# Attention with minus the row maximum added in PSUM, and the state stage's weights prepared by GpSimd

## The reference

```
x = x + attention(_gn(x))
  win = windows of 7x7 pixels            # 16 images x 16 windows, 49 tokens each
  q, k, v = win @ w_qkv + b_qkv          # 4 heads of 8 channels
  attn = softmax(q @ k.T * 8**-0.5)      # 49 x 49 per window and head
  x1 = (attn @ v) @ w_proj + b_proj
x = x + state_stage(_gn(x))              # grouped 1x1, 3x3 depthwise conv,
                                         # in_proj, conv1d, x_proj, dt_proj,
                                         # scan over 784 steps, out_proj, ...
```

## Time and profile before

| | us |
|---|---|
| median of 3 runs | 478.54 |
| lowest, highest | 476.59, 478.87 |
| profiled execution, its own time | 475.85 |
| span of the profiled execution | 474.1 |

### The profile page before, as it was taken

One profiled execution on the slowest core, in us unless ns is written; L12 is line 12 of the kernel. 1 busy time (PEld: TensorE's weight loads), 2 busy tenths in 40 slices (PEclk: granted clock), 3 DMA queues, 4 the chain that ended last, 5 costly groups with the idle time before them and its releaser, 6 DMA issues. The chain is left out here.

```text
span 474.1 us, 10021 instructions
## 1 busy us (share of the span) xinstructions
PE 351.1 (74%) x3480; PEld 230.4 (49%) x3480; DVE 365.1 (77%) x679; ACT 299.8 (63%) x583; POOL 233.9 (49%) x217
## 2 busy tenths in 40 slices
PE   5149888896789785985877647666795829888885
PEld 4037676675665332142233213222483519877774
DVE  3799999999797388799787999997576685544443
ACT  4327788887785899578758946347985253333432
POOL 4526868775673324966972999567081130000000
PEclk9997999998899999599897885768999668999999
DMA  6110000000223231022000000000030000111111
...
DMA packets 24044, 10.29 MB, mean 22 GB/s; under 512 B 20576, under 2 KB 22368, under 8 KB 24016
## 3 DMA queue, kind: packets, MB, share of 16 engines
...
q0 software_dynamic: 128, 0.01, 0.2%
...
## 5 line engine op out<-in xcount | busy, mean ns | idle before, releaser
L480 POOL TENSOR_TENSOR Pr<-Pr,rc 128x392 f32<-128x392 f32 x64 | 54.4, 883 | 32.2 <-DVE rc L1826 32.2
L511 POOL TENSOR_TENSOR YA<-YA,hC 128x784 f32<-128x784 f32 x27 | 51.7, 1914 | 32.4 <-DVE hC L1910 31.5
L1349 PE MATMUL pair<-BCf,sel 96*128 96x392 bf16 x128 | 38.4, 394 | 35.0 <-DVE Hs L1894 30.8
L1894 DVE TENSOR_TENSOR_SCAN Hs<-dA,pair 128x784 f32<-128x784 f32 x32 | 57.1, 1785 | 1.0
L1193 PE MATMUL pair<-ident,Pr 128*128 128x128 f32 x256 | 41.1, 293 | 13.2 <-ACT PT L715 9.0
L1349 PEld LDWEIGHTS pair<-BCf,sel 96*128 96x128 bf16 x128 | 10.2, 105 | 74.0 <-issue 71.6
L1193 PEld LDWEIGHTS pair<-ident,Pr 128*128 128x128 f32 x256 | 29.2, 146 | 25.1 <-ACT PT L715 15.8
L1887 DVE TENSOR_TENSOR pair<-DU,pair 128x784 f32<-128x784 f32 x32 | 31.1, 973 | 10.6 <-PE pair L1349 10.3
L715 ACT ACTIVATE PT<-pair 128x392 f32<-128x392 f32 x64 | 31.4, 497 | 5.9 <-PE pair L1193 5.6
L724 ACT ACTIVATE Pr<-Ts 128x392 f32<-128x392 f32 x64 | 32.5, 536 | 3.4 <-DVE Ts L1810 3.4
L1804 DVE TENSOR_REDUCE mx<-pair 128x8 f32<-128x392 f32 x64 | 32.6, 550 | 1.6 <-PE pair L1150 1.4
...
## 6 DMA issues: line engine op xcount, KB each, us to landing
...
NB<-in_L_conv_x_proj_w SPq DMA_DIRECT2D x4, 3.0 KB
DW<-in_L_conv_dw SPq DMA_DIRECT2D x4, 1.1 KB
vec<-in_L_conv_b_qkv POOLq DMA_DIRECT2D x3, 0.5 KB, 5.8
...
```

Source lines behind the costliest of these rows:

```text
L480: eng.tensor_tensor(pg, pg, bcast(rc[:, g, :], 2, WT), ALU.mult).then_inc(pn_r, 1)
L511: eng.tensor_tensor(y, y, hC[:, n % NHC, :], ALU.add).then_inc(g_ya, 1)
L1349: ins = eng.matmul(SPREAD[s][:, columns(h)], sel[:, n, :], upper(BCf[:, c % 2, s, columns(h)]), start=True, stop=True)
L1894: eng.tensor_tensor_scan(Hs[:, n % 2, :], dA[:, n % NA, :], SPREAD[0], 0.0, ALU.mult, ALU.add).then_inc(v_s, 1)
```

## The change

The subtraction of the maximum leaves VectorE. The maxima of two groups (16 numbers a partition) are cut into an upper and a lower bf16 piece (`upper_piece`, `lower_piece`, into `MP`), TensorE turns them onto 32 rows of bank 7 (`turn_max`), VectorE copies these out as bf16 (`turned_max`, into `MT`), and a matmul of `MT` with a constant of 0 and -1 (`msel`) adds minus the maximum to the scores where they lie in PSUM (`shift`, with `start=False`). The exponential reads PSUM (`exponent`), and the banks are free for the next scores when the exponential is done (`exp_r` in place of `sub_r`). `Ts` is gone.

The weights of the state stage: GpSimd does the fifteen products into `W8X` and `NB` ahead of its first strip; VectorE keeps the block transpose, the mean and two small steps; GpSimd then makes the copies behind strip 0, `BD` behind strip 1 and `WBC` behind strip 2.

The diff, without changed declarations of semaphores and the waits `sub_r` to `exp_r` at the conv and delta matmuls:

```diff
--- before.py
+++ after.py
...
@@ -234,6 +236,11 @@
         s_out = [sem("s_out0"), sem("s_out1")]
 
         block = ctx.enter_context(nc.Block())
+
+        QP = 64 + WT
+
+        def shift_rows(part):
+            return banks[7][0:32, 256 + P * part:256 + P * part + QP]
 
         def strip(s):
             return bass.ds(s * ST, ST)
@@ -455,7 +462,23 @@
             eng.wait_ge(s_ev, 8)
             for m in (xw, Qw, Vst, Pr):
                 eng.memset(m[:], 0.0).then_inc(s_mk2, 1)
+            eng.memset(MT[:], 0.0).then_inc(s_mk2, 1)
+            eng.wait_ge(s_mk, 5)
+            eng.tensor_tensor(mrow[:, :], ident[0:32, 0:16], ident[0:32, 16:32], ALU.add).then_inc(s_mk2, 1)
+            eng.wait_ge(s_mk2, 6)
+            eng.tensor_scalar(msel[:, :, :, :].rearrange("p g m k -> p (g m) k"), bcast(mrow[:, :], 2, WT), -1.0, None, ALU.mult).then_inc(s_mk2, 1)
             eng.wait_ge(s_mk2, 1)
+            eng.wait_ge(s_sel, 1)
+            loaded(eng, 1)
+            for k, dst in ((0, W8X[:, :]), (1, NB[:, 1, :]), (2, NB[:, 2, :])):
+                ins = eng.tensor_tensor(dst.rearrange("p (h i) -> p h i", h=4), bcast(W8[:, k, :], 1, 4), bcast(mask8[:, :], 2, 8), ALU.mult)
+            ins.then_inc(s_hf, 1)
+            for k in range(3):
+                eng.tensor_scalar(NB[:, 4 + k, :], WIN[:, 0, :], C1[:, k:k + 1], None, ALU.mult)
+            eng.wait_ge(s_hf, 2)
+            for k in range(9):
+                ins = eng.tensor_scalar(NB[:, 7 + k, :], W8X[:, :], DW[:, k:k + 1], None, ALU.mult)
+            ins.then_inc(s_hf, 1)
 
             def pool_att(s, par):
                 nxt = not isinstance(s, int) or s + 1 < NS
@@ -479,8 +502,24 @@
                         pg = Pr[:, par, g, :, 0:WT]
                         eng.tensor_tensor(pg, pg, bcast(rc[:, g, :], 2, WT), ALU.mult).then_inc(pn_r, 1)
 
-            for s in (-1, 0, 1, 2):
-                pool_att(s, s % 2)
+            pool_att(-1, 1)
+            pool_att(0, 0)
+            eng.wait_ge(s_sel, 2)
+            eng.tensor_copy(W4[:, U_Z:U_DL, :], TB[:, 0:U_DL - U_Z, :]).then_inc(s_hf, 1)
+            for x in range(3):
+                rows = slice(C * x, C * x + C)
+                eng.wait_ge(s_hf, 4 + x)
+                eng.tensor_copy(W3[rows], TB[rows, U_DL - U_Z + x:16:3, :]).then_inc(s_hf, 1)
+            eng.wait_ge(s_hf, 7)
+            pool_att(1, 1)
+            eng.tensor_tensor(BD[:, U_Z:U_CV, :].rearrange("p u (g c) -> p u g c", g=G), bcast(W4[:, U_Z:U_CV, :], 2, G),
+                              bcast(bcast(bd[:, :], 1, U_CV - U_Z), 3, C), ALU.mult)
+            pool_att(2, 0)
+            for s in range(2):
+                for q in range(3):
+                    ins = eng.tensor_tensor(WBC[:, s, C * q:C * q + C].rearrange("p (g n) -> p g n", g=G),
+                                            bcast(TB[:, 17, R + DS * s:R + DS * s + DS], 1, G), bcast(bd[:, :], 2, DS), ALU.mult)
+            ins.then_inc(s_hf, 1)
             eng.memset(XP[:, :, :], 0.0).then_inc(s_bd, 1)
             with eng.Fori(0, 6) as it:
                 pool_att(it * 2 + 3, 1)
@@ -718,17 +757,17 @@
                 def exponent(g):
                     if not cur:
                         return
-                    eng.wait_ge(sub_r, 4 * s + g + 1)
+                    eng.wait_ge(sh_r, 4 * s + g + 1)
                     if not fixed or s >= 2:
                         eng.wait_ge(t_r, 4 * (s - 2) + g + 1)
-                    eng.activation(Pr[:, par, g, :, 0:WT], Ts[:, g, :, :], ACT.Exp).then_inc(exp_r, 1)
+                    eng.activation(Pr[:, par, g, :, 0:WT], banks[g][:, 0:392].rearrange("p (m k) -> p m k", k=WT), ACT.Exp).then_inc(exp_r, 1)
 
                 turned_out(0)
+                turned_out(1)
+                turned_out(2)
                 exponent(0)
-                turned_out(1)
+                turned_out(3)
                 exponent(1)
-                turned_out(2)
-                turned_out(3)
                 exponent(2)
                 exponent(3)
                 if nxt:
...
@@ -1150,8 +1189,25 @@
                                 ins = eng.matmul(banks[g][64 * half:64 * half + 64, 196 * pair:196 * pair + 196],
                                                  Qw[C * g:C * g + C, par, 2 * pair + half, :],
                                                  Km[C * g:C * g + C, par, 2 * pair + half].rearrange("p h k -> p (h k)"),
-                                                 start=True, stop=True)
+                                                 start=pair == 0, stop=False, skip_group_check=True)
                     ins.then_inc(s_r, 1)
+
+                def turn_max(part):
+                    if not cur:
+                        return
+                    eng.wait_ge(max_r, 10 * s + (5, 8)[part])
+                    if part == 0 and (not fixed or s >= 2):
+                        eng.wait_ge(ao_r, s - 1)
+                    eng.matmul(shift_rows(part), MP[:, part, :], upper(ident[:, 0:QP]), start=True, stop=True,
+                               skip_group_check=True).then_inc(mt_r, 1)
+
+                def shift(part):
+                    if not cur:
+                        return
+                    eng.wait_ge(max_r, 10 * s + 9 + part)
+                    for g in (2 * part, 2 * part + 1):
+                        eng.matmul(banks[g][:, 0:392], MT[:, part, :], msel[:, g % 2].rearrange("p m k -> p (m k)"),
+                                   start=False, stop=True, skip_group_check=True).then_inc(sh_r, 1)
 
                 scores(0)
                 scores(1)
@@ -1196,6 +1252,8 @@
                 def av():
 
                     eng.wait_ge(ring_r, base + G)
+                    if cur:
+                        eng.wait_ge(max_r, 10 * s + 10)
                     if not fixed or s >= 2:
                         eng.wait_ge(ao_r, s - 1)
                     for w in range(NW):
@@ -1209,11 +1267,16 @@
                 if prv:
                     transposes(0)
                     transposes(1)
+                turn_max(0)
                 if early:
                     early()
                 if prv:
                     transposes(2)
+                shift(0)
+                turn_max(1)
+                if prv:
                     transposes(3)
+                shift(1)
                 if prv2:
                     project()
                 if late:
...
@@ -1742,41 +1806,21 @@
                 return eng.tensor_tensor(BD[:, u0:u1, :].rearrange("p u (g c) -> p u g c", g=G), bcast(W4[:, u0:u1, :], 2, G),
                                          bcast(bcast(bd[:, :], 1, u1 - u0), 3, C), ALU.mult)
             eng.tensor_scalar(vec[:, V_BQS:V_BQS + 1], vec[:, V_BQ:V_BQ + 1], SCALE, None, ALU.mult)
-            eng.tensor_reduce(mask8[:, :], m16[:, :].rearrange("p (g h) -> p h g", g=G), AX.X, ALU.add)
+            eng.tensor_reduce(mask8[:, :], m16[:, :].rearrange("p (g h) -> p h g", g=G), AX.X, ALU.add).then_inc(s_sel, 1)
             spread_weights(U_Q, U_P + 1)
             gn_apply(0, lambda j: XN[:, T * j:T * j + T])
 
 
-            loaded(eng, 1)
-            link(eng.tensor_tensor(maskz[:, :], m8[:, 0:4], m8[:, 4:8], ALU.add))
-
-            for k, dst in ((0, W8X[:, :]), (1, NB[:, 1, :]), (2, NB[:, 2, :])):
-                ins = eng.tensor_tensor(dst.rearrange("p (h i) -> p h i", h=4), bcast(W8[:, k, :], 1, 4), bcast(mask8[:, :], 2, 8), ALU.mult)
-            link(ins)
-            for k in range(3):
-                eng.tensor_scalar(NB[:, 4 + k, :], WIN[:, 0, :], C1[:, k:k + 1], None, ALU.mult)
-            for k in range(9):
-                ins = eng.tensor_scalar(NB[:, 7 + k, :], W8X[:, :], DW[:, k:k + 1], None, ALU.mult)
-            link(ins)
+            eng.wait_ge(s_hf, 3)
             link(eng.transpose(TB[:, :, :].rearrange("p u c -> p (u c)"), NB[:, :, :].rearrange("p u c -> p (u c)")))
             assert chain[0] == TRB
 
             link(eng.tensor_reduce(omean[:, :], TB[:, 3, :], AX.X, ALU.add))
             link(eng.tensor_scalar(omean[:, :], omean[:, :], 1.0 / C, None, ALU.mult))
             link(eng.tensor_scalar(TB[:, 3, :], TB[:, 3, :], omean[:, 0:1], None, ALU.subtract))
-            eng.tensor_copy(W4[:, U_Z:U_DL, :], TB[:, 0:U_DL - U_Z, :])
-            link(eng.tensor_copy(W4[:, U_CV:NU, :], TB[:, U_DL - U_Z:16, :]))
-            for x in range(3):
-                rows = slice(C * x, C * x + C)
-                eng.tensor_copy(W3[rows], W4[rows, U_CV + x:NU:3, :])
             eng.wait_ge(s_wd, 1)
             eng.tensor_copy(W4[:, U_DL, :], banks[7][:, 0:C])
-            link(eng.tensor_tensor(vec[:, V_BZF:V_BZF + 1], vec[:, V_BZ:V_BZ + 1], banks[7][:, C:C + 1], ALU.add))
-            spread_weights(U_Z, U_CV)
-            for s in range(2):
-                for q in range(3):
-                    eng.tensor_tensor(WBC[:, s, C * q:C * q + C].rearrange("p (g n) -> p g n", g=G),
```

(45 more changed lines are left out.)

20 lines of the change are left out of this document (12 added, 8 removed).

## The result

| | before | after |
|---|---|---|
| median of 5 runs, us | 476.59 | 531.38 |
| lowest, highest | 470.71, 478.87 | 527.24, 532.97 |
| span of the profiled execution | 474.1 | 530.2 |
| mean granted clock | 0.901 | 0.847 |

The ratio is 1.120, with an interval of 1.110 to 1.130. The prediction was 496, with a range of 484 to 505: slower was right, the size was not.

A forecast was written before the change was run, and what follows sets the result against it. VectorE looked like the bound, 6.5 us a strip, beside an equally long 6.60 loop through GpSimd and TensorE. Terms -0.6 + 0.4 + 0.9 + 19.6 + 0.3 - 1.0 = +19.6 us led to 496, range 484 to 505.

The forecast's parts named there:

- Two round trips in series: VectorE's second copy and then its residual each wait for TensorE in every strip, idling about 0.9 and 1.1 us.
- T0 to T1: In a strip, from VectorE's first copy of turned maxima to its second: 1.01 us.
- a): Start of a strip on VectorE, from the reciprocal to the next first maximum: 0.87 us.
- b): VectorE's four maxima and four bf16 pieces up to the first copy: 2.65 us, bounds 2.3 to 3.1.
- T1 to P: In a strip, from VectorE's second copy of turned maxima to TensorE's projection: 0.75 us.
- P to X: In a strip, from TensorE's projection to VectorE's residual: 0.65 us.
- the 6.60 loop: Before: reciprocal, GpSimd's normalisations, last transposes, projection, residual, sums take 6.60 us a strip; TensorE work before the projection adds to it.
- the fifteen products: Small weight products that GpSimd does ahead of its first copy of `xw` and `Km`: 4.5 to 5.5 us.
- the later `xw` and `Km`: GpSimd's copies come some 0.5 us late behind strip 2's six products; cost taken as 0.3, ends 0 and 1.8.
- the port wait added to b): Lower pieces reading two SBUF tensors wait for GpSimd's instruction in hand: 0.45 us a strip, ends 0 and 1.2.
- the DU row: Trace evidence for waiting: product DU on VectorE took 0.97 us with GpSimd idle, 2.64 beside a GpSimd addition.
- rival 4: TensorE's extra waits bring half clock, doubling some 1.8 us in a third of strips: +8, 504 us; chance 0.15.

The follow-up runs named there:

- experiment 2: The changed kernel with the maxima kept in PSUM, so no piece reads two SBUF inputs and no cast of a piece reads SBUF: 500.12 us, ratio 1.045.
- experiment 10: The kernel before plus four unused bf16 matmuls of 256 columns on TensorE just ahead of the projection: 482.14 us, ratio 1.014.
- experiment 1: The kernel before with only the weights part of the change, moved to GpSimd, attention as before: 478.91 us against 478.31, ratio 1.003.
- experiment 8: The kernel before plus the four bf16 pieces a strip on VectorE, read from maxima in SBUF and used by nobody: 499.77 us, ratio 1.048.
- experiment 11: The changed kernel without its two lower pieces a strip, the casts still reading the maxima from SBUF: 509.09 us, ratio 1.069.
- experiment 5: The changed kernel plus 20 spare bf16 matmuls of 128 columns where TensorE waits for the pieces, strips 2 to 15: 527.13 us, ratio 1.103.
- experiment 6: The changed kernel with one round trip a strip: all maxima in PSUM, one cast, one lower piece, one turning, one copy, projection before shifts: 491.06 us, ratio 1.029.
- experiment 7: The one-round-trip version of the changed kernel without its lower piece, subtracting only the maximum rounded to bf16: 489.16 us, ratio 1.029.

## Why the prediction was right in direction and wrong in size

Right, by its own steps:
- the mechanism. Two round trips in series with VectorE idle at the second copy and at the residual: 0.75 and 2.16 after, 0.75 and 1.41 with the port out of the way (foreseen: 0.9 and 1.1). T0 to T1 was put at 1.01 and is 1.01 to 1.04. Without the port the whole strip is 8.18 where 7.68 was forecast, some 7 us over 14 strips. The difference is a) +0.15, b) +0.08, T1 to P +0.16, P to X +0.11. In a) the prediction took 0.87 from one short strip; the mean of the seven strips before is 1.07. T1 to P and P to X lack the weight load of the projection, which no longer lies beside other work (experiment 2).
- the 6.60 loop: experiment 10.
- ScalarE's exponential from PSUM: 510 ns after, 537 before. It cost nothing.
- the fifteen products: 4.7 (23.93 to 28.61), put at 4.5 to 5.5; and nothing behind attention but the shift. (The terms around them were too kind: the first maximum came 0.14 earlier, counted from the load, and not 0.6; and for the later `xw` and `Km` the sum had 0.3 where experiment 1 lost 2.6 in strips 1 to 4.)

The step that failed is the port wait added to b). I read the DU row as a wait to the end of GpSimd's instruction in hand, which experiments 8 and 11 bear out (in the DU row itself the sum of remainder and own length is 2.77, and 2.64 was measured), and then sized it at 0.45 a strip, for two lower pieces in seams between normalisations. It is 1.58 (L to T0 4.31 against 2.73). Two things were wrong in it. The casts wait as the lower pieces do, and are the larger part (0.51 each over the 0.175 that they take from PSUM, the lower pieces 0.24 each). The prediction had the Trainium skill's sentence for that, SBUF — State Buffer, section "Who interferes with whom", that casts too can take the shared ports, and set it aside as the upper end, 1.2, which was too low as well. The trace agrees with the page, the fill of `XP` included: the page lets a cast in two-port mode, in which VectorE uses the shared ports as well, contend with GpSimd, with no exception for instructions that only write. It makes that exception for a VectorE instruction with two SBUF inputs; no run here tests that. And the forecast put the pieces beside normalisations of 0.81, while in each of the six strips between 70 and 137 one piece was held to the end of `Km`, the longest instruction that GpSimd has there: the second cast in four of them (1.04 to 1.25), the first lower piece in two (1.37, as at 108.44, just after `Km` was taken up at 108.27). Against the forecast this is 1.13 a strip, 16 us over 14 strips.

The second failure is rival 4, set at a chance of 0.15 and at a third of the strips; the forecast's own sum had the clock at nothing. It came with the first: with TensorE's waits for the pieces (2.09 in the strip shown, 0.33 in the same place of experiment 2) the clock was 0.82 over all seven strips, where it had been 1.00 and is 1.00 again in experiment 2. From T1 to the next first maximum the changed kernel needs 5.66, experiment 2 needs 4.44: 1.22 a strip, 17 us over 14. This is the clock: the two strips with the full clock take what experiment 2 takes (experiment 5). Rival 4's price was right: it had 1.8 for a strip in half clock, and strips 3, 5 and 8, at 0.51 to 0.53, are 1.76, 2.20 and 2.11 longer than in experiment 2. Its share was wrong: five of seven strips were hit. Why those five and not the other two is not shown. Nor is it shown how much of the port's part hangs on the clock in turn: L to T0 is 3.89 and 3.70 in the two strips with full clock, 1.15 and 0.96 over the same strips of experiment 2 (experiment 8 had 1.15 a strip), and 4.33 to 4.90 in the others.

Together: 7 for the longer series, 16 for the port, 17 for what came with the clock, 40 of the 38.3 by which the last reciprocal is late against the forecast (57.9 against 19.6). Small terms go both ways. Strip 0 took 6.90 from maximum to reciprocal, not 5.6, since its pieces met GpSimd's `Km` too. The load was 1 us late in that execution. Strip 12, with the table loads, took 10.61 before (the reciprocals at 113.21 and 123.82) and 11.03 after (160.59 and 171.62): 0.4 more where a quiet strip grew by 4.23, so it gave back 3.8 where 1.0 was put down.

No version tried with the shift in it beats the kernel before. The best, experiments 6 and 7, are 2.9% slower: even with one trip and no port the turning stands in TensorE's queue behind work that waits for others.
